# First attention: the projection of q directly behind that of the context's keys, the turned inverse sums behind both

## The chip, the cores and the metric

The kernel runs on one core of a Trainium2 chip. The metric is the device time of one launch in microseconds (us): 1333.4 us before the change, the median of three runs from 1332.63 to 1336.6 us. One further execution was profiled; all rows below are from it.

## What is computed

The input x is 32 entries of 128 tokens by 128 channels, with a context of 120 tokens per entry. Four blocks follow one another, each added to x. Only the first one is touched:

```
x = x + _L0_xattn_ref(ctx_1024, _layernorm(x), mask, ...)      # the first attention
x = x + _L0_ffn_ref(_layernorm(x), ...)
x = x + _L1_xattn_ref(_layernorm(x), ctx_1024, ctx_1024, ...)
x = x + _L1_ffn_ref(_layernorm(x), ...)

# inside the first attention, 8 heads of 64:
q = latents @ Wq                                   # latents: the normed tokens of x
k, v = split(concatenate([ctx, latents]) @ Wkv)    # 120 + 128 = 248 keys
q = l2norm(q) * q_scale;  k = l2norm(k) * k_scale
attn = softmax(where(mask, q @ k.T * 8, -max))
out = layer_norm((attn @ v) @ Wo) 
```

## The kernel before, in words

`l0_attention` works through the 32 entries one at a time, in a software pipeline written out by hand. Each engine has its own list of steps, `body(n, par)`, which `run_steps` calls for n from -2 to 33; a step for entry n + 2 (the projections), one for n + 1 (turning q and the keys, the first scores) and those for n (softmax and the product with the values) stand side by side in one body. Each engine takes its list strictly in the order written; semaphores with names like `q_proj` or `vl_copied` count entries done, and a step begins with its waits. The eight PSUM banks are shared by the steps under fixed rules; bank 7, for one, holds in turn the values of x, q, and the keys of x.

TensorE's steps that matter here (names of the functions, with the lines of their matmuls):

- `project_kc` (L334): the context's keys of entry n + 2, 512 wide, into bank 6. It waits for `kvT_made`, that is for ScalarE's two copies of the turned inputs (L496, L497).
- `turn_sums` (L426): two transposes of `r_wide`, the inverse sums of the softmax of entry n repeated over 64 columns, into bank 4. It waits for `sum_repeated` (VectorE, L624) and for `pt0_copied` (ScalarE's copy L541, which empties bank 4). u is the half of the heads, 0 or 1; the change touches u = 0.
- `project_q` (L340): q of entry n + 2, 512 wide, into bank 7. It waits for `kvT_made` and for `vl_copied`, since bank 7 still holds the values of x of entry n + 1 until ScalarE has copied them (L489, `copy_values_x`).
- `multiply_v` (L441), `turn_probs0` (L407), `turn_kc` (L352), `project_kl` (L345, the keys of x, into bank 7 once `q_copied` is there), `turn_probs1` (L418), `turn_kl` (L367), `turn_q` (L360), `multiply_v` and `turn_sums` of the other half, `values_c` (L374), `scores` (L392, L397), `values_x` (L381), `scores`, `project` (L450).

ScalarE's list runs: copy of the context's values (L483), four exponentials of half 0 (L533), copy of the output projection (L553), the two copies that make `kvT` (L496, L497), `copy_pt0` (L541), `copy_values_x` (L489), four exponentials of half 1, `copy_sums` of half 0 (L547, waits for the turned sums), the copies of the context's keys and of q (L504, twice), `copy_pt0`, `copy_kcT` (L518), the copy of the keys of x (L504), the squares (L512), `copy_qT` (L315), `copy_sums` of half 1. A product in float32 stands in the trace as two loads of weights and two matmuls; a transpose as one of each.

The waits of the three steps that change their neighbours, as the code has them:

```
def project_q(m):
    if there(m):
        wait(pe, s["kvT_made"], m + 1)
        wait(pe, s["vl_copied"], m)
def turn_sums(n, u):
    if there(n):
        wait(pe, sum_repeated[u], n + 1)
        wait(pe, pt0_copied[u], n + 1)
```

Of the kernel before, what the change touches and what calls it, by code (L numbers as in the profile page):

```python
# [30 lines left out]
def wait(eng, sem, value):  # L31

    if isinstance(value, int) and value <= 0:
        return
    eng.wait_ge(sem, value)  # L35
# [103 lines left out]
def there(n):  # L139

    return not isinstance(n, int) or 0 <= n < B


def l0_attention(nc, psum, X, stats6, mean, rstd, mhalf, small, ident, ident_bf, ones, cols,
# [6 lines left out]
    with ExitStack() as sems, ExitStack() as st:  # L151
# [169 lines left out]
        with nc.Block() as block:  # L321
            @block.tensor
            def _(pe):
                def turn_inputs(m):
                    if there(m):
                        wait(pe, s["ln_made"], m + 1)
                        wait(pe, s["vc_copied"], m)
                        pe.transpose(psum[:, 6, 0:C], ln_c[0:C, :], ident[0:C, 0:C])
                        pe.transpose(psum[:, 6, P:2 * P], ln_x[:, :], ident[:, :]).then_inc(s["ln_turned"], 1)

                def project_kc(m):
                    if there(m):
                        wait(pe, s["kvT_made"], m + 1)
                        pe.matmul(psum[0:C, 6, :], kvT[:, 0:C], wkv[:, 0:INNER], start=True, stop=True).then_inc(s["kc_proj"], 1)  # L334
# [5 lines that stand above are left out]
                        pe.matmul(psum[:, 7, :], kvT[:, C:K], wq[:, :], start=True, stop=True).then_inc(s["q_proj"], 1)  # L340

                def project_kl(m):
                    if there(m):
                        wait(pe, s["q_copied"], m + 1)
                        pe.matmul(psum[:, 7, :], kvT[:, C:K], wkv[:, 0:INNER], start=True, stop=True).then_inc(s["kl_proj"], 1)  # L345

                def turn_kc(m):
                    if there(m):
                        wait(pe, s["normed"], m + 1)
                        wait(pe, s["kc_copied"], min(m + 2, B) if isinstance(m, int) else m + 2)  # L350
                        for c in range(4):
                            tr = pe.transpose(psum[:, 6, c * C:(c + 1) * C], qkn[0:C, 1, c * P:(c + 1) * P], ident[0:C, 0:C])  # L352
                        tr.then_inc(s["kcT_turned"], 1)
# [22 lines left out]
                def values_x(m):  # L376
                    if there(m):
                        wait(pe, s["qT_copied"], m)
                        wait(pe, s["qT_scaled"], m)
                        wait(pe, s["kl_copied"], m + 1)  # L380
                        pe.matmul(psum[:, 7, :], kvT[:, C:K], wkv[:, INNER:], start=True, stop=True).then_inc(s["vl_proj"], 1)  # L381

                def scores(n, u, par):
                    if there(n):
                        if u == 0:
                            wait(pe, s["qT_copied"], n + 1)
                            wait(pe, s["qT_scaled"], n + 1)
                            wait(pe, s["klT_copied"], n + 1)
                            wait(pe, s["keep_copied"], n + 1)
                        wait(pe, exp_done[u], n)  # L390
                        for r in range(2):
                            pe.matmul(psum[:, 2 * u + r, 0:2 * K], first_row[64 * r:64 * r + 64, :],  # L392
                                      keep_now[par][64 * r:64 * r + 64, :].unsqueeze(1).broadcast_to([64, 2, K]),
                                      start=True, stop=False, skip_group_check=True)
                        for j in range(2):
                            for r in range(2):
                                mm = pe.matmul(psum[:, 2 * u + r, j * K:(j + 1) * K], QT[par][64 * r:64 * r + 64, 2 * u + j, :],  # L397
                                               KT[par][64 * r:64 * r + 64, 2 * u + j, :], start=False, stop=True,
                                               skip_group_check=True)
                        mm.then_inc(scored[u], 1)  # L400

                def turn_probs0(n, u):
                    if there(n):
                        wait(pe, exp_done[u], n + 1)
                        wait(pe, r_copied[1 - u], n if u == 0 else n + 1)
                        for j in range(4):
                            tr = pe.transpose(psum[0:C, 4, j * P:(j + 1) * P], probs[u][:, j, 0:C], ident[:, :])  # L407
                        tr.then_inc(pt0_turned[u], 1)

                def turn_probs1(n, u):  # L410
                    if there(n):
                        wait(pe, exp_done[u], n + 1)
                        if u == 0:
                            wait(pe, s["projection_taken"], n)
                        else:
                            wait(pe, out_scaled[0], n + 1)
                        for j in range(4):
                            tr = pe.transpose(psum[:, 5, j * P:(j + 1) * P], probs[u][:, j, C:K], ident[:, :])  # L418
                        tr.then_inc(pt1_turned[u], 1)
# [5 lines that stand above are left out]
                        for b in range(2):  # L425
                            tr = pe.transpose(psum[:, 4, b * P:(b + 1) * P],  # L426
                                              r_wide[u][:, 2 * b:2 * b + 2, :].rearrange("p h w -> p (h w)"), ident[:, :])
                        tr.then_inc(r_turned[u], 1)

                def multiply_v(n, u, par):  # L430
                    if there(n):
                        wait(pe, pt0_copied[u], n + 1)
                        wait(pe, pt1_copied[u], n + 1)
                        if u == 0:
                            wait(pe, s["vc_copied"], n + 1)
                            wait(pe, s["vl_copied"], n + 1)
                        for j in range(2):
                            for part, V, rows in ((0, VC, C), (1, VL, P)):
                                for r in range(2):
                                    h = 4 * u + 2 * j + r  # L440
                                    mm = pe.matmul(psum[HD * r:HD * r + HD, 5, j * P:(j + 1) * P], V[par][0:rows, h * HD:(h + 1) * HD],  # L441
                                                   probsT[u][0:rows, part, 2 * r + j, :], start=(part == 0), stop=(part == 1),
                                                   skip_group_check=True)
                        mm.then_inc(pv_done[u], 1)

                def project(n):
                    if there(n):
                        wait(pe, out_scaled[1], n + 1)
                        for c in range(4):
                            mm = pe.matmul(psum[:, 5, 0:D], outT[:, c, :], wo[:, c, :], start=(c == 0), stop=(c == 3))  # L450
                        mm.then_inc(s["projected"], 1)

                def body(n, par):
                    values_x(n + 1)
                    scores(n, 1, par)
                    project(n - 1)
                    turn_inputs(n + 2)
                    turn_probs0(n, 0)
                    turn_probs1(n, 0)
                    project_kc(n + 2)  # L460
                    turn_sums(n, 0)
                    project_q(n + 2)
                    multiply_v(n, 0, par)
                    turn_probs0(n, 1)
                    turn_kc(n + 1)
                    project_kl(n + 2)
                    turn_probs1(n, 1)
                    turn_kl(n + 1)
                    turn_q(n + 1)
                    multiply_v(n, 1, par)  # L470
                    turn_sums(n, 1)
                    values_c(n + 2)
                    scores(n + 1, 0, 1 - par)

                run_steps(pe, body)

            @block.scalar
# [1731 lines left out]
```

## Time and profile before

| | |
|---|---|
| median of 3 runs | 1333.4 us (1332.63 to 1336.6) |
| the profiled execution | 1335.86 us, its span 1333.7 us |
| TensorE (PE) | matmuls on record for 1230.1 us, 92% of the span |
| loads of weights (PEld) | 879.3 us, 66% |
| VectorE (DVE), ScalarE (ACT), GpSimd (POOL) | 70%, 60%, 44% |
| first attention | about 28 to 510 us of the span |
| granted TensorE clock, mean | 0.969 of full speed |

The profiled execution's own time is 2.5 us above the median; the span leaves out another 2.2 us around it. "Busy" on PE covers each matmul from its start until its modelled end, and matmuls overlap, so a PE that is busy all the time may still have paused between two of them; the pauses show in the starts of the rows, and in the idle time of PEld.

### The profile page before, as it was taken

The page shows a single profiled execution, that of the slowest core. Times are in us where ns is not written, and L with a number is a line of the kernel's source. Part 1 is how long each engine was busy: PE and PEld are TensorE (multiplying, and loading weights), DVE is VectorE, ACT ScalarE, POOL GpSimd, SP SyncE. Part 2 cuts the span into 40 slices and gives each one's busy share as a digit, 9 for nine tenths or more (in the row PEclk, how much of TensorE's full clock was granted, in tenths as well). Part 3 has the DMA queues.
Part 4 walks back from the last instruction along what each step waited for, and adds up shares of the span by engine and source line. Part 5 has one row for each costly group of instructions (what it writes and reads, how often), then busy time and mean ns, then how long its engine had stood idle before and what let it go on. Part 6 is the DMA issues. An engine that isn't in the chain of part 4 may idle for free. (4 is left out here: it accounts for less than half of the span.)

```text
span 1333.7 us, 37978 instructions
## 1 busy us (share of the span) xinstructions
PE 1230.1 (92%) x13719; PEld 879.3 (66%) x13719; DVE 927.5 (70%) x2003; ACT 798.9 (60%) x2101; POOL 588.9 (44%) x673
## 2 busy tenths in 40 slices
PE   1899999999999995978999899989999979999996
PEld 0466666666666663436777777768888847777775
DVE  6476676677677673766999889979999955343431
ACT  0578878878878862325777677756666633333332
POOL 3577566666656655104223332343333223333343
PEclk9899999999999997987999899989999979999998
DMA  8000000000000000000000002000000000000000
GB/s 216 13 1 1 0 0 0 0 0 0 0 0 0 0 1 1 0 4 10 11 9 8 10 10 69 3 2 1 0 0 0 0 1 9 9 8 8 8 11 16
DMA packets 22740, 14.71 MB, mean 11 GB/s; under 512 B 6378, under 2 KB 21610, under 8 KB 22540
## 3 DMA queue, kind: packets, MB, share of 16 engines
q1 hardware_dynamic: 22520, 13.75, 3.8%
q8 instruction: 43, 0.70, 0.2%
q14 instruction: 29, 0.24, 0.1%
q10 hardware_dynamic: 148, 0.01, 0.0%
HBM read 11.66 MB, written 2.10 MB: 10 GB/s over the span
## 5 line engine op out<-in xcount | busy, mean ns | idle before, releaser
L690 POOL TENSOR_TENSOR r_norm<-ssm,mhalf 128x24 f32<-128x24 f32 x32 | 134.9, 4215 | 162.7 <-DVE ssm L595 162.7
L1767 POOL TENSOR_TENSOR pair_QX<-pair_qT,own_slots 128x512 f32<-128x512 f32 x64 | 66.7, 1041 | 257.7 <-ACT pair_qT L1579 257.7
L1985 ACT ACTIVATE moe_hid<-psum 128x512 f32<-128x512 f32 x128 | 76.4, 598 | 137.5 <-PE psum L1919 137.5
L1525 PE MATMUL psum<-ident,pair_probs 128*120 128x128 f32 (+1 forms) x1024 | 154.6, 285 | 0.7 <-ACT pair_probs L1594 0.6
L533 ACT ACTIVATE l_probs<-psum,l_n_max 128x248 f32<-128x248 f32 x256 | 117.2, 481 | 57.7 <-DVE l_n_max L613 57.7
L2143 POOL TENSOR_TENSOR moe_acc<-moe_acc,moe_prod 128x512 f32<-128x512 f32 x64 | 81.3, 1271 | 147.4 <-DVE moe_prod L2099 147.4
L1594 ACT ACTIVATE pair_probs<-psum,pair_n_max 128x120 f32<-128x120 f32 (+1 forms) x512 | 137.7, 380 | 10.4 <-DVE pair_n_max L1636 5.0
L1929 PEld LDWEIGHTS psum<-w,moe_hid 128*128 128x128 f32 x1024 | 123.1, 192 | 26.8 <-issue 26.8
L2099 DVE TENSOR_TENSOR moe_prod<-psum,moe_combine 128x512 f32<-128x512 f32 x64 | 44.3, 692 | 135.8 <-PE psum L1929 135.7
L1525 PEld LDWEIGHTS psum<-ident,pair_probs 128*120 128x120 f32 (+1 forms) x1024 | 111.3, 141 | 28.6 <-issue 11.9
L1462 ACT COPY pair_probsT<-psum 120x512 f32<-120x512 f32 (+1 forms) x128 | 77.7, 607 | 86.4 <-PE psum L1525 86.2
L1929 PE MATMUL psum<-w,moe_hid 128*128 128x128 f32 x1024 | 123.4, 275 | 0.0
L1919 PE MATMUL psum<-moe_moe_hT,w 128*128 128x512 f32 x256 | 122.5, 606 | 0.0
L1536 PE MATMUL psum<-pair_probsT,V 120*32 120x128 f32 (+1 forms) x2048 | 107.2, 281 | 0.3 <-DVE X L1678 0.3
L1539 PE MATMUL psum<-pair_probsT,ONE 120*32 120x128 f32 (+1 forms) x2048 | 104.3, 275 | 0.0
L1462 DVE COPY pair_probsT<-psum 120x512 f32<-120x512 f32 (+1 forms) x128 | 87.2, 681 | 4.7 <-PE psum L1525 4.6
L697 POOL TENSOR_TENSOR qkn<-qk,r_norm 128x1536 f32<-128x1536 f32 x32 | 88.4, 2762 | 2.5
L1602 ACT ACTIVATE pair_probs<-pair_probs 128x960 f32<-128x960 f32 (+1 forms) x64 | 67.0, 1047 | 35.9 <-DVE pair_probs L1654 35.9
L1636 DVE TENSOR_REDUCE pair_n_max<-psum 128x8 f32<-128x960 f32 (+1 forms) x64 | 76.1, 1189 | 8.8 <-PE psum L1514 8.8
L640 DVE TENSOR_TENSOR outT<-psum,r_spread 128x256 f32<-128x256 f32 x64 | 26.9, 420 | 78.8 <-PE psum L441 73.3
L613 DVE TENSOR_REDUCE l_n_max<-psum 128x4 f32<-128x992 f32 x64 | 76.3, 1192 | 6.4 <-PE psum L397 2.4
L1514 PE MATMUL psum<-pair_kT,pair_QX 32*128 32x120 f32 (+1 forms) x2048 | 77.2, 287 | 0.0
(292 smaller groups left out, 2925.3 us busy)
## 6 DMA issues: line engine op xcount, KB each, us to landing
X<-x_in SPq DMA_DIRECT2D x8, 256.0 KB, 4.6
out_dram<-moe_acc SPq DMA_DIRECT2D x32, 64.0 KB, 1.5
CT<-ctx_in SPq DMA_DIRECT2D x8, 240.0 KB, 5.5
pair_cT<-ctxT_in SPq DMA_DIRECT2D x32, 60.0 KB, 1.8
w<-w_in SPq DMA_DIRECT2D x1, 1024.0 KB, 5.0
wm<-wm_in SPq DMA_DIRECT2D x1, 768.0 KB, 4.3
wp<-wp_in SPq DMA_DIRECT2D x1, 768.0 KB, 6.6
wkv<-wkv_in SPq DMA_DIRECT2D x1, 512.0 KB, 5.3
```

What stands on the lines that cost most here:

```text
L533: e = act.activation(probs[u][:, h, :], psum[:, 2 * u + h // 2, (h % 2) * K:(h % 2 + 1) * K], ACT.Exp, bias=n_max[u][:, h:h + 1], accum_ou ...
L690: pool.tensor_tensor(r_norm[:, :], ssm[:, :], mhalf[:, 0:3 * H], ALU.pow).then_inc(s["norm_inverted"], 1)
L697: pool.tensor_tensor(qkn[:, :, :].rearrange("p a (h d) -> p (a h) d", d=HD), qk[:, :, :].rearrange("p a (h d) -> p (a h) d", d=HD), r_norm ...
L1462: copy(probsT[0:K, g, :, :], psum[0:K, 4 + g % 2, :].rearrange("k (j q) -> k j q", j=4)).then_inc(copied[g], 1)
L1514: mm = pe.matmul(psum[:, t, s * K:(s + 1) * K], QX[par][32 * t:32 * t + 32, s, :], kT[par][32 * t:32 * t + 32, 0:K], start=False, stop=(s ...
L1525: tr = pe.transpose(psum[0:K, 4 + g % 2, j * P:(j + 1) * P], probs[par][:, 4 * g + j, 0:K], ident[:, :])
L1536: pe.matmul(psum[32 * tile:32 * tile + 32, 6, 0:P], V[par][0:K, g * P + 32 * tile:g * P + 32 * tile + 32], probsT[0:K, g, tile, :], start= ...
L1539: mm = pe.matmul(psum[32 * tile:32 * tile + 32, 6, P:2 * P], ONE[0:K, 32 * g:32 * g + 32], probsT[0:K, g, tile, :], start=False, stop=(g = ...
L1594: e = act.activation(probs[par][:, h, 0:K], psum[:, h // 4, (h % 4) * K:(h % 4 + 1) * K], ACT.Exp, bias=n_max[par][:, h:h + 1])
L1919: pe.matmul(psum[:, 2 + i % BANKS, :], w1[:, e, half * P:(half + 1) * P], hT[par][:, :], start=True, stop=True).then_inc(hidden[i], 1)
L1929: mm = pe.matmul(psum[:, 5 + e % 2, b * D:(b + 1) * D], hid[i % RING][:, b * P:(b + 1) * P], w2[:, i, :], start=(half == 0), stop=(half == ...
L2143: pool.tensor_tensor(a[:, :, :], a[:, :, :], prod[e % 2][:, :, :], ALU.add).then_inc(summed[e], 1)
```

## The change

`project_q(n + 2)` and `turn_sums(n, 0)` change places in TensorE's list. No instruction is added or removed, and no wait is changed.

```
--- before.py
+++ after.py
@@ -458,8 +458,8 @@
                     turn_probs0(n, 0)
                     turn_probs1(n, 0)
                     project_kc(n + 2)
+                    project_q(n + 2)
                     turn_sums(n, 0)
-                    project_q(n + 2)
                     multiply_v(n, 0, par)
                     turn_probs0(n, 1)
                     turn_kc(n + 1)
```

TensorE, the middle of one body (psum<-wkv,kvT is the product for the context's keys, psum<-wq,kvT that for q, r_wide the repeated inverse sums):

```order
 L418 MATMUL psum<-ident,l_probs 128x128 x4
 L334 MATMUL psum<-wkv,kvT 120x512
-L426 MATMUL psum<-ident,r_wide 128x128 x2
 L340 MATMUL psum<-wq,kvT 128x512
+L426 MATMUL psum<-ident,r_wide 128x128 x2
 L441 MATMUL psum<-l_probsT,VC 64x128 x2
 L441 MATMUL psum<-l_probsT,VL 64x128 x2
```

The two transposes moved from ahead of the product for q to behind it. The same piece stands eight times in the code that is built (six written-out bodies and the two of the loop), and in the execution it runs for 30 entries.

ScalarE's list beside it, the same before and after, from the copies that make kvT to the copy of the keys of x:

```order
 L497 ACTIVATE kvT<-psum,cols 128x128
 L541 COPY l_probsT<-psum 120x512
 L489 COPY VL<-psum 128x512
 L533 ACTIVATE l_probs,l_sums<-psum,l_n_max 128x248 x4
 L547 COPY r_spread<-psum 128x256
 L504 COPY qk<-psum 120x512
 L504 COPY qk<-psum 128x512
 L541 COPY l_probsT<-psum 120x512
 L518 COPY KT<-psum 128x4x120
```

Nothing moved here. L489 is what the product for q waits for, L547 what waits for the turned sums, and the second L504 what empties q's bank.

## Rows read from the trace of the kernel before

**Rows 1.** The page: busy us, share of the span, instructions.
```profile
PE 1230.1 (92%) x13719; PEld 879.3 (66%) x13719; DVE 927.5 (70%) x2003; ACT 798.9 (60%) x2101; POOL 588.9 (44%) x673
```

**Rows 2.** Stretches in the first attention: busy us by engine, granted clock, DMA share, GB/s.
```profile
100.00:200.00 100.00, 99.93 (x723) 64.48 (x722) 69.80 (x147) 79.43 (x215) 65.86 (x52) 1.00 0.00 1
200.00:300.00 100.00, 99.95 (x725) 64.75 (x725) 70.02 (x145) 79.21 (x215) 62.94 (x50) 1.00 0.00 0
```

**Rows 3.** The product for q (L340), whole run: count, ns min/median/max, first and last start.
```profile
L340 PEld LDWEIGHTS psum<-wq,kvT x64: 190/192/337, 28.9 to 476.9; 128*128 128x128 f32 x64
```

**Rows 4.** The first product (L334), 100 to 340 us, the same columns.
```profile
L334 PEld LDWEIGHTS psum<-wkv,kvT x34: 179/180/183, 100.9 to 331.7; 128*120 128x120 f32 x34
```

**Rows 5.** Timeline of one entry: start us, us, engine, line [idle before <-releaser].
```profile
215.75 0.45 ACT L497 ACTIVATE kvT<-psum,cols 128x128 f32<-128x128 f32 x1
...
216.25 0.28 PEld L334 LDWEIGHTS psum<-wkv,kvT 128*120 128x120 f32 x2 [0.26 <-ACT kvT L497]
216.25 1.12 PE L334 MATMUL psum<-wkv,kvT 128*120 128x512 f32 x2
...
216.56 0.60 ACT L489 COPY VL<-psum 128x512 f32<-128x512 f32 x1
216.79 0.14 PEld L426 LDWEIGHTS psum<-ident,r_wide 128*128 128x128 f32 x1 [0.25 <-issue]
217.04 0.49 ACT L533 ACTIVATE l_probs<-psum,l_n_max 128x248 f32<-128x248 f32 x1
217.21 0.38 PE L426 MATMUL psum<-ident,r_wide 128*128 128x128 f32 x2
217.21 0.14 PEld L426 LDWEIGHTS psum<-ident,r_wide 128*128 128x128 f32 x1 [0.28 <-issue]
217.32 0.30 PEld L340 LDWEIGHTS psum<-wq,kvT 128*128 128x128 f32 x2
...
217.43 1.02 PE L340 MATMUL psum<-wq,kvT 128*128 128x512 f32 x2
...
218.38 0.44 PE L441 MATMUL psum<-l_probsT,VC 120*64 120x128 f32 x4
```

**Rows 6.** The same entry, ScalarE's copies behind the exponentials, and TensorE there.
```profile
218.82 0.42 ACT L547 COPY r_spread<-psum 128x256 f32<-128x256 f32 x1
...
219.07 1.14 ACT L504 COPY qk<-psum 120x512 f32<-120x512 f32 x2
...
219.41 0.65 PE L407 MATMUL psum<-ident,l_probs 128*120 128x128 f32 x4
...
219.90 0.58 PE L352 MATMUL psum<-ident,qkn 120*128 120x120 f32 x4
...
220.26 0.30 PEld L345 LDWEIGHTS psum<-wkv,kvT 128*128 128x128 f32 x2
...
221.23 0.60 PE L418 MATMUL psum<-ident,l_probs 128*128 128x128 f32 x4
```

**Rows 7.** The same entry, the turning of q (L360) behind the copy of the keys of x.
```profile
221.48 0.59 ACT L504 COPY qk<-psum 128x512 f32<-128x512 f32 x1 [0.32 <-PE psum L345]
221.66 0.60 PE L367 MATMUL psum<-ident,qkn 128*128 128x128 f32 x4
...
222.18 0.42 PEld L360 LDWEIGHTS psum<-ident,qkn 128*128 128x128 f32 x4 [0.16 <-issue]
```

**Rows 8.** Who waited for whom, 100 to 340 us: us in total, times, longest.
```profile
POOL r_norm L690 <- DVE ssm L595: 79.7, 17, 5.0
```

More of the change, by code:

```diff
@@ L460, in body @@
                     project_kc(n + 2)
+                    project_q(n + 2)
                     turn_sums(n, 0)
-                    project_q(n + 2)
                     multiply_v(n, 0, par)
```

## The prediction

> **What bounds the kernel now.** I read the page first, then the stretches of the first attention, then one entry of it row by row. The page gives TensorE 92% of the span [rows 1]. In the first attention it is on record all the time, 99.9 us of every 100, at the full granted clock of 1.00 (2.4 GHz), while ScalarE has 79% and VectorE 70% [rows 2]. GpSimd waits 79.7 us in 17 entries for VectorE, so it has time to spare [rows 8]. One entry takes (331.7 - 100.9) / 16 = 14.4 us: the first and last start of L334 in the stretch, for 34 loads, two per entry, the second a tenth behind the first [rows 4]. So the time of this stage is the sum of what TensorE streams and of its short pauses, and I read those from the distance between starts. What the change costs or saves per entry counts in full, unless another engine's fixed chain takes it up. L340 has 64 loads, so 32 entries [rows 3]; for the first two no inverse sums are turned, which leaves 30.
>
> **The change part by part.** Nothing is added or removed: two transposes and one product of 512 columns change places. What has to be priced is which of them meets its waits at what time.
>
> *How TensorE goes through the place now.* ScalarE finishes kvT at 215.75 + 0.45 = 216.20, the load for L334 starts at 216.25, and the first transpose of the sums at 217.21 [rows 5]. The load for that transpose starts at 216.79, as the second pass of L334 begins, 0.42 to 0.43 before 217.21; so a pass takes 0.43, a product 0.86, and what is left of the 0.96 from load to successor is 0.10, the load that stands in the open because it had to wait. Behind it there is no gap: the two transposes take 217.43 - 217.21 = 0.22, the product for q runs from 217.43 to about 218.29, and L441 starts at 218.38 after 0.09 for the switch to its shape.
>
> *The product for q, moved forward.* It may not start before ScalarE has emptied its bank: L489 runs from 216.56 to 216.56 + 0.60 = 217.16 [rows 5]. TensorE would be free for it at 217.21, but wants the load before that, at 216.79 (where the sums' load stands now); it can't have it. The transposes hid this wait: they needed nothing from L489 and filled 0.22. From the end of a ScalarE copy to the load it releases I see 0.05 (kvT, 216.20 to 216.25; and the copy of q, which ends at 219.07 + 1.14 = 220.21, to the load of L345 at 220.26 [rows 6]) and 0.11 (the keys of x, 221.48 + 0.59 = 222.07 to the load of L360 at 222.18 [rows 7]). L360 waits for two semaphores, as L340 does, while L334 and L345 wait for one; so I take 0.11. The Trainium skill, page "Perfetto Trace Analysis", section "Identifying Dependency Chains", says that an instruction waiting for several engines may get a semaphore instruction ahead of it; that is one way to read the difference, and no number here hangs on it.
>
> So the load for q starts at 217.16 + 0.11 = 217.27, and its columns stream from 217.37, against 217.21 for what stands there now: **0.16 us later**. With a hand-over of 0.05 it is 0.10 later. Then 0.86 and 0.22 as before, and L441 starts at 218.54 instead of 218.38. Nothing behind the waiting load is blocked for another reason; the sums and L441 are ready, they are only late with it.
>
> *The transposes of the sums, moved back.* They now end at 217.21 + 0.38 = 217.59; then at 217.37 + 0.86 + 0.38 = 218.61. Their reader, L547, starts at 218.82, behind ScalarE's exponentials [rows 6]. Even with a hand-over of 0.11 that is in time: cost nothing. If the exponentials were shorter by more than 0.1 us, this copy, and the two L504 behind it, would slip. The product for q ends earlier than now, but its copy stands behind the same exponentials: gain nothing.
>
> *What takes some of it back.* L345 is held by the copy of q: the four transposes of L352 begin at 219.90 and are through after about 0.41 (0.58 less one transpose's length of 0.27, plus 0.10 for its columns), at 220.31, while the load at 220.26 lets L345 stream from 220.36 only, and L418 follows at 221.23. This chain on ScalarE (L489, exponentials, L547, L504 twice) hangs on nothing that the change moves, so a TensorE that comes 0.16 later loses this 0.05 again. Every other wait of the entry (0.26 for kvT, 0.1 for the keys of x at L360) starts from a product of TensorE itself, moves with it, and takes up nothing. GpSimd's spare time hides its part.
>
> The sum: 0.16 - 0.05 = **0.11 us per entry, times 30 = 3.3 us**. The profiled execution's 1335.86 us would become 1339.2; against the median of 1333.4 us, which I forecast, it is **1336.7 us**. The bounds: 0.10 - 0.05 = 0.05 per entry gives 1.5 us, 0.16 with nothing taken back gives 4.8 us.
>
> **A rule that speaks against a cost.** The trace shows the load of the sums' transpose at 216.79 beside the second pass of L334, both on all 128 rows, and the transpose 0.42 later with no gap [rows 5]; so loads do hide here, and one that has to wait does not. The Trainium skill, page "TensorE: Matmul & The Clock Gate", section "The mechanism", says that a load of weights overlaps running matmuls only when its group of rows is another one. By that rule the load would be in the open in either order and only the late hand-over would count; rival 1 has its time.
>
> **The rivals.**
> 1. *The move is free.* The load for q costs the same wherever it stands, so the wait costs 217.27 - 217.21 = 0.06, and L345's 0.05 takes that back: 0.01 x 30 = 0.3 us, 1333.7. For it: L489 ends 0.05 before TensorE wants the bank. Against it: the hidden load at 216.79.
> 2. *Slower by more than can be overlooked.* The load for q stands in the open with its whole recorded length, 0.19 [rows 3], instead of 0.10: columns from 217.46, 0.25 late, 0.20 after what is taken back, times 30 = 6.0 us, 1339.4. It decides from 0.13 us per entry on (4.0 us in all). Against it: L334's load is recorded with 0.18 too [rows 4], and its successor comes after 0.96, not 1.04.
> 3. *Faster.* The load side sits idle for 0.25 and 0.28 around the sums' transposes [rows 5]. If the second of these were a true pause between two kinds of matmul, and two products back to back spared it, an entry would gain 0.28 - 0.11 = 0.17, times 30 = 5.1 us: 1328.3. Against it: the starts of the matmuls leave no room for a pause.
> 4. *The order on TensorE is not what decides*, because ScalarE's chain sets the entry. Then nothing changes: 1333.4. Against it: TensorE's waits that ScalarE releases are themselves released by TensorE.
>
> **How the numbers follow.** A measurement of this kernel tells about 0.3%, 4.0 us, from no change. Forecast: chance 0.57; with its bounds of 1.5 to 4.8 us and runs that differ by a few us, about a quarter of it lies above 4.0. Rival 1: 0.16. Rival 2: 0.17. Rival 3: 0.04. Rival 4: 0.06. So faster 0.04; slower 0.17 + 0.15 = 0.32; within 0.3% the rest, 0.64. The later stages are untouched and only start some 3 us later. The likeliest is 1336.7 us. The range of 1333.0 to 1340.0 us holds the forecast with both bounds, rival 1 and 4, and rival 2 at its price.
>
> **What would show it.** In the profile of the changed kernel L334 is followed by the load of L340, about 1.02 us behind the load of L334 (217.27 - 216.25) and 0.11 behind the end of L489, not 0.5 behind L334's; L426 about 1.98 behind it, L441 2.29 instead of 2.13. L345's load no longer starts 0.05 behind the end of the copy of q but later. L547 keeps its place at 2.57 behind L334's load. The entry takes 14.5 us instead of 14.4, and the stage ends some 3 us later. If the entry takes 14.4 as before, rival 1 or 4 holds, and the place of L441 tells which; if L441 comes at 2.38 or later, rival 2; if L441 comes before 2.13, rival 3. A start of L547 behind 2.57 would mean that I mispriced the late sums.

## The result, and the profile after

The change makes the kernel slower by a quarter of a per cent: 1337.43 us, the median of 18 runs (1334.11 to 1339.34), against 1334.06 us, the median of 18 runs of the kernel before. The ratio is 1.0024, with a 95% interval from 1.0017 to 1.0031. That is 2.3 to 4.1 us, where 3.3 were forecast. The forecast of 1336.7 us started from the 1333.4 us of three runs; from the 1334.06 of 18 the same 3.3 give 1337.4. The 18 runs resolve a difference that lies below the 0.3% set as the bound of "no change".

The page of the changed kernel shows nothing of it but the span; TensorE's share is the same [rows 1]:

```profile
span 1336.7 us, 37978 instructions
PE 1230.6 (92%) x13719; PEld 878.4 (66%) x13719; DVE 923.2 (69%) x2003; ACT 801.7 (60%) x2101; POOL 588.4 (44%) x673
```

Nor do the stretches of the first attention, which answer to [rows 2] (busy us by engine, granted clock, DMA share, GB/s). TensorE is on record all the time with and without the longer pause, and at the same clock:

```profile
100.00:200.00 100.00, 99.93 (x716) 64.05 (x716) 68.09 (x145) 79.25 (x210) 64.98 (x52) 1.00 0.00 1
200.00:300.00 100.00, 99.95 (x724) 64.62 (x720) 68.21 (x146) 80.57 (x217) 62.11 (x49) 1.00 0.00 0
```

The starts tell it. The loads of L334 from 100 to 340 us (count, ns min/median/max, first and last start), and those of L340 in the whole run, answer to [rows 4] and [rows 3]:

```profile
L334 PEld LDWEIGHTS psum<-wkv,kvT x34: 179/180/183, 101.1 to 333.8; 128*120 128x120 f32 x34
...
L340 PEld LDWEIGHTS psum<-wq,kvT x64: 186/189/337, 29.9 to 480.2; 128*128 128x128 f32 x64
```

34 loads are 17 entries, so 16 distances and the 0.1 us between the two loads of one product: (333.8 - 101.1 - 0.1) / 16 = 14.54 us per entry, against (331.7 - 100.9 - 0.1) / 16 = 14.42 before. 0.12 us more, 30 times, is 3.6 us. (From 101.1 to the last load of L334 at 479.2 us it is 378.1 us, before from 100.9 to 475.8 374.9: 3.2 us more for 26 entries. The first 70 us of the stage differ by 0.8 us the other way between these two single executions, which was not looked into.) This length of an entry is what the experiments below are read by, since it is steadier than a time: it is worked out in the same way for each.

One entry, from the timeline of the changed kernel (start us, us, engine, line, [idle before <-releaser]), answers to [rows 5, 6]:

```profile
202.38 0.45 ACT L497 ACTIVATE kvT<-psum,cols 128x128 f32<-128x128 f32 x1
...
202.88 0.28 PEld L334 LDWEIGHTS psum<-wkv,kvT 128*120 128x120 f32 x2 [0.23 <-ACT kvT L497]
...
203.19 0.61 ACT L489 COPY VL<-psum 128x512 f32<-128x512 f32 x1
...
203.91 0.30 PEld L340 LDWEIGHTS psum<-wq,kvT 128*128 128x128 f32 x2 [0.74 <-issue]
203.94 1.10 PE L340 MATMUL psum<-wq,kvT 128*128 128x512 f32 x2
...
204.87 0.38 PE L426 MATMUL psum<-ident,r_wide 128*128 128x128 f32 x2
...
205.19 0.44 PE L441 MATMUL psum<-l_probsT,VC 120*64 120x128 f32 x4
...
205.45 0.42 ACT L547 COPY r_spread<-psum 128x256 f32<-128x256 f32 x1
...
205.70 1.15 ACT L504 COPY qk<-psum 120x512 f32<-120x512 f32 x2
...
206.71 0.57 PE L352 MATMUL psum<-ident,qkn 120*128 120x120 f32 x4
...
207.02 0.30 PEld L345 LDWEIGHTS psum<-wkv,kvT 128*128 128x128 f32 x2
...
207.98 0.60 PE L418 MATMUL psum<-ident,l_probs 128*128 128x128 f32 x4
```

Counted from L334's load, in us, before (from [rows 5, 6], with L334 at 216.25) and after:

| | before | after | forecast |
|---|---|---|---|
| the copy of the values of x (L489) ends | 0.91 | 0.92 | as before |
| load of the product for q (L340) | 1.07 | 1.03 | 1.02 |
| first transpose of the sums (L426) | 0.96 | 1.99 | 1.98 |
| first product with the values (L441) | 2.13 | 2.31 | 2.29 |
| copy of the turned sums (L547) | 2.57 | 2.57 | 2.57 |
| load for the keys of x (L345) | 4.01 | 4.14 | later than 4.01 |
| L418, behind it | 4.98 | 5.10 | 0.11 later |

The load for q stands 0.11 us behind the end of the copy that it waits for, and not 0.42 ahead of its columns as the load of the transposes did. At L441 the entry is 0.17 to 0.18 behind; from L345 on it is 0.12 behind, since that load no longer waits for the copy of q (which ends at 205.70 + 1.15 = 206.85) but follows the transposes of L352.

### The profile page after: what moved, and what is told of

It reads as the page before. It is cut to its first block and busy times, and to the rows that moved or that the text cites. A ratio compares the mean times of both kernels' runs of the same rounds, so it can differ in the third digit from the quotient of the medians.

```text
span 1336.7 us, 37978 instructions
## 1 busy us (share of the span) xinstructions
PE 1230.6 (92%) x13719; PEld 878.4 (66%) x13719; DVE 923.2 (69%) x2003; ACT 801.7 (60%) x2101; POOL 588.4 (44%) x673
## 5 line engine op out<-in xcount | busy, mean ns | idle before, releaser
L613 DVE TENSOR_REDUCE l_n_max<-psum 128x4 f32<-128x992 f32 x64 | 76.2, 1191 | 6.6 <-PE psum L397 2.6
```

## The experiments

Ten kernels were run, each against the kernel before on the same chip. An entry of each is worked out from the loads of L334, as above.

### The wait taken away: ScalarE copies the values of x first

The edit, on the changed kernel, in ScalarE's list:

```
-                    copy_pt0(n, 0)
                     copy_values_x(n + 1, 1 - par)
+                    copy_pt0(n, 0)
```

> The changed kernel, but ScalarE copies the values of x (L489) ahead of the probabilities (L541), so the bank for q is free some 0.47 us earlier. My theory (the product for q waits for that copy and its load then stands in the open): the wait is gone, L426 about 1.82 us behind L334's load and L441 at 2.13 as before the change, L345's load 0.05 behind the copy of q again, an entry 14.42 us, ratio to before 1.000. Rival (the place of the transposes between the two products is what matters, not the wait): L441 stays at 2.30, an entry 14.54 us, ratio 1.0024.

Measured: 1334.05 us, ratio 0.9998 (0.9988 to 1.0009); the entry (331.6 - 100.9 - 0.1) / 16 = 14.41. From its timeline:

```profile
201.67 0.58 ACT L489 COPY VL<-psum 128x512 f32<-128x512 f32 x1
201.83 0.28 PEld L334 LDWEIGHTS psum<-wkv,kvT 128*120 128x120 f32 x2 [0.23 <-ACT kvT L497]
...
202.37 0.19 PEld L340 LDWEIGHTS psum<-wq,kvT 128*128 128x128 f32 x1 [0.25 <-issue]
202.78 1.02 PE L340 MATMUL psum<-wq,kvT 128*128 128x512 f32 x2
...
203.64 0.38 PE L426 MATMUL psum<-ident,r_wide 128*128 128x128 f32 x2
```

The load for q now stands 0.54 behind L334's and its columns follow at 0.95, the places that the sums had in the kernel before. The order of the change is kept, and its cost is gone. The order as such costs nothing; the wait does.

### The same swap in the kernel before

> The kernel before, with the same swap on ScalarE. Now the transposes of the sums meet the late copy (L541 ends about 0.90 us behind L334's load). My theory: their load starts at 1.01 instead of 0.53, their columns 0.11 late, 0.05 of it taken back at L345: an entry 14.48 us, plus 1.8 us in all, ratio 1.0013. Rival (the order on TensorE alone matters): nothing changes, ratio 1.000.

The edit is the same, made on the kernel before. Now the copy of the probabilities, which the sums wait for, is the late one. Measured: 1336.61 us, ratio 1.0016 (1.0005 to 1.0027); the entry (333.8 - 101.9 - 0.1) / 16 = 14.49.

```profile
203.65 0.60 ACT L541 COPY l_probsT<-psum 120x512 f32<-120x512 f32 x1
204.37 0.20 PEld L426 LDWEIGHTS psum<-ident,r_wide 128*128 128x128 f32 x2 [0.74 <-issue]
204.40 0.41 PE L426 MATMUL psum<-ident,r_wide 128*128 128x128 f32 x2
```

The copy ends at 204.25, the load follows 0.12 later and 1.02 behind L334's load at 203.35. L441 starts 2.25 behind L334's load instead of 2.13, so the sums' columns start at 0.96 + 0.12 = 1.08: ahead of transposes the load stands 0.06 in the open, not 0.10 as ahead of a product. The 0.12 less the 0.05 at L345 is the loss of the entry, 0.07 us, 0.06 forecast: it appears in the old order. The two runs cross: with ScalarE's old order TensorE's old order is the better one by 0.12, with ScalarE's new order the new one is, by 0.08.

### The price of the second wait

```
                 def project_q(m):
                     if there(m):
-                        wait(pe, s["kvT_made"], m + 1)
                         wait(pe, s["vl_copied"], m)
```

> The changed kernel, but the product for q waits for the copy of the values alone; that kvT is made was waited for by the product just ahead of it on the same engine. My theory (two waits cost 0.11 us from the end of the copy to the load, one costs 0.05): q's load 0.96 instead of 1.03 behind L334's, L441 at 2.24, L345's 0.05 still taken back, an entry 14.48 us, ratio to before 1.0012. Rival (the hand-over has nothing to do with the number of waits): as the change, ratio 1.0024, load at 1.03.

Measured: 1336.83 us, ratio 1.0013 (1.0002 to 1.0024); the entry (333.7 - 102.0 - 0.1) / 16 = 14.48. Line numbers are one lower here (L339 is the product for q, L488 the copy of the values of x):

```profile
203.32 0.28 PEld L334 LDWEIGHTS psum<-wkv,kvT 128*120 128x120 f32 x2 [0.23 <-ACT kvT L496]
...
204.29 0.30 PEld L339 LDWEIGHTS psum<-wq,kvT 128*128 128x128 f32 x2 [0.68 <-ACT VL L488]
204.29 1.12 PE L339 MATMUL psum<-wq,kvT 128*128 128x512 f32 x2
```

The load comes 0.97 behind L334's instead of 1.03, and half of what the change costs is gone. So a wait that was long met was part of this step's hand-over. The profile tells the two cases apart too: with one wait it names ScalarE's copy as what ended the idle time, with two it says "issue". The number of waits alone is not the rule, though. In `project_q` the late wait is the second of the two in the code; the last two sections have a step whose first wait is the late one, and there the hand-over is 0.05 with both waits in place.

### What came back at the keys of x

Both of the next kernels let VectorE copy the turned sums of half 0 (L547 before), so that ScalarE reaches the copy of q earlier:

```
+                def copy_sums0(n):
+                    if there(n):
+                        wait(dve, r_turned[0], n + 1)
+                        wait(dve, out_scaled[1], n)
+                        dve.tensor_copy(r_spread[:, :, :], psum[:, 4, 0:2 * P]...).then_inc(r_copied[0], 1)
```

> The kernel before, but VectorE instead of ScalarE copies the turned sums of half 0 (L547), so ScalarE reaches the copy of q some 0.25 us earlier. My theory (L345 is held about 0.05 us by the copy of q, and by nothing else): its columns start 0.05 earlier, an entry 14.36 us, ratio to before 0.9988. Rival (the copy of q holds nothing): 14.42, 1.000.

> The changed kernel with the same move of the copy to VectorE. My theory (the change costs 0.17 at the product for q, and 0.05 of it came back at L345 because that was held anyway): with the hold gone on both sides nothing comes back, an entry 14.53 us as in the change, 0.17 more than the kernel before with the same move, ratio to before 1.0024. Rival (the 0.12 between before and change is all that the late product costs): 0.12 more than that kernel, 14.48, ratio 1.0015.

Measured: on the kernel before 1333.41 us, ratio 0.9994 (0.9984 to 1.0004), the entry (332.1 - 102.1 - 0.1) / 16 = 14.37; on the change 1336.68 us, ratio 1.0026 (1.0016 to 1.0036), the entry (334.7 - 102.0 - 0.1) / 16 = 14.54. On the first, L345's load comes 3.96 behind L334's, where it was 4.01:

```profile
202.72 0.28 PEld L334 LDWEIGHTS psum<-wkv,kvT 128*120 128x120 f32 x2 [0.23 <-ACT kvT L497]
...
205.29 1.12 ACT L504 COPY qk<-psum 120x512 f32<-120x512 f32 x2
...
206.68 0.30 PEld L345 LDWEIGHTS psum<-wkv,kvT 128*128 128x128 f32 x2
```

With the hold gone on both sides the orders are 0.17 apart, not 0.12. So the late product for q costs 0.17, and 0.05 of it fell into a wait that the kernel before had anyway. The times alone would not have shown the 0.05 (1.5 us in 30 entries); the entries do.

### The lesson used elsewhere: the sums of the other half

TensorE pauses at L360 for ScalarE's copy of the keys of x [rows 7]. On the kernel before:

```
                     turn_kl(n + 1)
+                    turn_sums(n, 1)
                     turn_q(n + 1)
                     multiply_v(n, 1, par)
-                    turn_sums(n, 1)
```

> The kernel before, but the turned sums of the other half stand ahead of the turning of q (L360), where TensorE pauses about 0.14 us for the copy of the keys of x. My theory (a short ready piece ahead of a step that waits hides the wait): the pause goes, the values product L374 starts 0.10 us earlier behind L334's load (7.72 instead of 7.82; the load behind the products with 64 columns is now its own 0.10 in the open), an entry 14.32 us, minus 3.0 us, ratio 0.9977. Rival (the pause is only moved: another wait from ScalarE or VectorE ends as late as before): an entry 14.42, ratio 1.000.

Measured: 1329.87 us, ratio 0.9968 (0.9955 to 0.998); the entry (330.9 - 101.7 - 0.1) / 16 = 14.32.

```profile
207.19 0.59 ACT L504 COPY qk<-psum 128x512 f32<-128x512 f32 x1 [0.32 <-PE psum L345]
...
207.38 0.60 PE L367 MATMUL psum<-ident,qkn 128*128 128x128 f32 x4
...
207.81 0.38 PE L426 MATMUL psum<-ident,r_wide 128*128 128x128 f32 x2
207.92 0.47 PEld L360 LDWEIGHTS psum<-ident,qkn 128*128 128x128 f32 x4
...
208.03 0.60 PE L360 MATMUL psum<-ident,qkn 128*128 128x128 f32 x4
```

The copy ends at 207.78, while TensorE is busy with the turned sums; the load of L360 follows at 207.92, 0.11 ahead of its first transpose. Nothing pauses: 0.43, 0.22 and then L360. The entry is 0.10 shorter, as worked out; that is 3.0 us in all, while the medians are 4.2 apart, with 3.0 inside the interval. It is the mirror image of the change: a short piece that is ready stands ahead of one that is not.

### kvT on VectorE: a miss

The largest pause of an entry is that of 0.26 ahead of L334 [rows 5]. Both copies that make kvT were given to VectorE, between its maximum (L613) and the inverse sums; the sums of the other half stand ahead of L360 as above.

```
                     maximum(n, 1)
+                    make_kvT(n + 2)
                     invert_sums(n, 0)
```

with, in `make_kvT`, `tensor_scalar(..., LNX_W, LNX_B, ALU.mult, ALU.add)` and its like for the tokens. It was run with TensorE's old order (first) and with that of the change (second).

> The kernel before with the sums of the other half ahead of the turning of q, and with both copies that make kvT on VectorE instead of ScalarE; ScalarE's list is shorter by two copies. My theory: the pause of 0.26 us ahead of L334 goes, and with it the hold at L345, an entry 14.32 - 0.26 - 0.05 = 14.01 us, minus 12 us in all, ratio 0.9908. Rival (VectorE, which now has the two copies ahead of the inverse sums and the other copies, ends later than TensorE needs it, and the pause comes back at the products with the values): 14.3 us, 0.997.

> The same with the order of the change, the product for q directly behind that for the context's keys. My theory (what the order costs is how far the copy of the values of x lies behind the moment the load for q could start): the copy ends about 0.63 us behind the place of L334's load as it is now, the load follows at 0.74 where it could start at 0.27, the columns at 0.84 instead of 0.70: 0.14 more than the same kernel with the old order, nothing taken back, an entry 14.15 us, ratio 0.994. Rival (with ScalarE's list shorter by two copies the values of x are copied in time): no difference between the two orders.

Measured: 1395.09 us, ratio 1.0472 (1.0432 to 1.0511), the entry (335.4 - 104.4 - 0.1) / 14 = 16.49; and 1407.09 us, ratio 1.0551 (1.0533 to 1.0569), the entry (328.9 - 106.2 - 0.1) / 13 = 17.12. Neither theory had this. Who waited for whom from 100 to 340 us, in the first of them (line numbers shifted: L622 is VectorE's copy into r_wide, L624 before), and one entry:

```profile
PEld psum L426 <- DVE r_wide L622: 37.6, 15, 2.5
...
PE psum L426 <- DVE r_wide L622: 25.0, 15, 1.7
```

```profile
217.54 0.40 DVE L581 TENSOR_SCALAR kvT<-psum,cols 128x120 f32<-128x120 f32 x1
...
217.86 0.40 DVE L582 TENSOR_SCALAR kvT<-psum,cols 128x128 f32<-128x128 f32 x1
...
218.14 2.76 POOL L696 TENSOR_TENSOR qkn<-qk,r_norm 128x1536 f32<-128x1536 f32 x1
...
218.38 2.67 DVE L622 COPY r_wide<-l_r_sums 128x256 f32<-128x256 f32 x1
...
221.10 0.20 PEld L426 LDWEIGHTS psum<-ident,r_wide 128*128 128x128 f32 x2 [2.50 <-DVE r_wide L622]
```

In the kernel before, the same copies, of both halves, with GpSimd beside them:

```profile
215.42 0.29 DVE L624 COPY r_wide<-l_r_sums 128x256 f32<-128x256 f32 x1
...
215.91 2.76 POOL L697 TENSOR_TENSOR qkn<-qk,r_norm 128x1536 f32<-128x1536 f32 x1
...
216.31 0.69 DVE L632 COPY l_probsT<-psum 128x512 f32<-128x512 f32 x1
...
219.90 0.47 POOL L721 TENSOR_TENSOR y_wb<-y_w,lnob 128x128 f32<-128x128 f32 x1
...
220.07 0.45 DVE L624 COPY r_wide<-l_r_sums 128x256 f32<-128x256 f32 x1
```

The copy of 128x256 took 2.67 us. In the kernel before that of half 0 takes 0.29, and it starts some 0.5 us ahead of GpSimd's qkn. Here the two kvT copies push it behind the start of qkn, and it ends at 221.05, 0.15 behind the end of qkn (220.90). The copy of the other half shows the same on a small scale in the kernel before: it starts beside GpSimd's y_wb, takes 0.45 and ends at 220.52, again 0.15 behind the end of y_wb (220.37). TensorE waits for the late copy with the sums.

In the second kernel the product for q goes ahead of the sums and TensorE waits less in one piece, yet it is slower still. What the order was forecast to cost there, 0.14, did not come: the copy of the values of x ends 0.73 behind L334's load, q's load follows at 0.85 and its columns at 0.96, where TensorE is free for them anyway. The difference lies in the granted clock, 0.95 from 100 to 350 us against 0.99 in the first. In the second kernel it falls to 0.50 of full speed (1.2 GHz) for some 3.4 us in every second entry (from 213.2 to 216.6 us, for one), seven times from 100 to 340 us, and such an entry takes 1.5 us longer; in the first it falls twice, and those entries take 1.6 to 1.7 longer. Without these falls the entries would be about 16.3 and 16.25 us, by my estimate from these numbers. Ahead of the fall at 213.2 TensorE stood still for 0.81 us for the sums and for 0.92 ahead of L441; one entry later it stood still for 0.81 and 1.02 (up to 229.29 and 230.75), and the clock stayed at full speed. Why it fell in one entry and not in the next stays open.

### The copy into r_wide on ScalarE

```
-                    dve.tensor_copy(r_wide[0] ..., r_sums[0] ...)     (invert_sums, u == 0)
+                    act.copy(r_wide[0] ..., r_sums[0] ...)            (repeat_sums0, ahead of exponentials(n, 1))
```

In both kernels ScalarE copies the values of x before the probabilities; they differ in TensorE's order alone, which is that of the change in the first and the old one in the second. (The expectation for the second speaks of ScalarE's old order. The kernel that ran has the new one.)

> As e8 (kvT on VectorE, the order of the change, the sums of the other half ahead of the turning of q), but the inverse sums of half 0 are repeated into r_wide by ScalarE instead of VectorE, behind the copies of the values of x and of the probabilities. My theory (the 2.7 us that VectorE's copy into r_wide took in e7 is a lock-out by GpSimd's qkn, which runs from 218.14 to 220.90 there and which the copy met only because the kvT copies pushed it back; with no such copy in that stretch the loss goes): an entry about 14.05 us, minus 11 us in all, ratio to before 0.992. Rival (VectorE simply has too much to do since it makes kvT): an entry stays above 15 us, ratio above 1.03.

> The same division of the work, with the old order (the sums ahead of the product for q) and ScalarE's old order of the two copies. Here the sums become ready last, at about 0.62 us behind the place of L334's load, where their load could start at 0.27. My theory (whichever of the two is ready first belongs ahead; here that is q): the columns of the sums start about 0.08 late, an entry 14.13 us, 0.08 more than e9, ratio 0.994. Rival (the old order is better by 0.12 whatever is ready first): 13.93 us.

Measured: 1327.59 us, ratio 0.9953 (0.9939 to 0.9966), the entry (328.7 - 101.8 - 0.1) / 16 = 14.18; and 1325.35 us, ratio 0.9939 (0.9923 to 0.9956), the entry (327.4 - 100.4 - 0.1) / 16 = 14.18. From the first:

```profile
214.70 0.40 DVE L591 TENSOR_SCALAR kvT<-psum,cols 128x128 f32<-128x128 f32 x1
...
214.99 2.76 POOL L707 TENSOR_TENSOR qkn<-qk,r_norm 128x1536 f32<-128x1536 f32 x1
...
215.16 0.28 PEld L334 LDWEIGHTS psum<-wkv,kvT 128*120 128x120 f32 x2 [0.18 <-DVE kvT L591]
215.30 0.41 ACT L532 COPY r_wide<-l_r_sums 128x256 f32<-128x256 f32 x1
```

From the second, where the sums stand ahead of the product for q:

```profile
213.83 0.28 PEld L334 LDWEIGHTS psum<-wkv,kvT 128*120 128x120 f32 x2 [0.18 <-DVE kvT L591]
...
213.97 0.41 ACT L532 COPY r_wide<-l_r_sums 128x256 f32<-128x256 f32 x1
...
214.43 0.14 PEld L426 LDWEIGHTS psum<-ident,r_wide 128*128 128x128 f32 x1 [0.32 <-ACT r_wide L532]
...
214.79 0.38 PE L426 MATMUL psum<-ident,r_wide 128*128 128x128 f32 x2
```

ScalarE's copy into r_wide takes 0.41 us in the middle of qkn, and the entry is 2.3 us shorter than that of the kernel above with the same order of TensorE (16.49) in the one case, 2.9 (17.12) in the other. VectorE's work is otherwise as it was: it lost a copy of 0.29 us. So it was the meeting of that copy with qkn, not the amount of VectorE's work. The size of the gain was off: 14.18 instead of 14.05, because VectorE needs 214.39 to 215.10, 0.71 us, for the two copies and ScalarE's pair took 0.80; L334 still pauses. For the same reason the difference of 0.08 between the two orders did not come: counted from L334's real place, the copy into r_wide ends at 0.55 and the copy of the values of x before it. The first order meets no wait. In the second the load of the sums comes at 0.60 instead of 0.54, still 0.36 ahead of its columns at 0.96: a load that is late and yet hidden costs nothing. Both kernels beat the kernel before and the change; whether the 0.9939 is really better than the 0.9953 is open, the intervals overlap and the entries are equal.

These rows also correct the price of the second wait. `turn_sums` waits first for the repeated sums, then for the copy of the probabilities. Here the first is the late one, and the load follows it by 0.05 (214.38 to 214.43); likewise by 0.05 (221.05 to 221.10) where VectorE made the sums late. In the swap on the kernel before, the second was the late one, and the same load came after 0.12. In `project_q` and `turn_q` (L360) the late wait is also the second. So the 0.06 was paid where the late wait stands behind another in the code, and not wherever a step has two. That writing the late wait first would save it without dropping any follows from this, but no kernel tried it.

## Why the prediction was right

- *What bounds the stage.* TensorE's own sequence does: each of the kernels that lengthened or shortened one pause there moved the entry by that pause, less what fell into the hold at L345, also where ScalarE had less to do (the entry of 14.54 with the sums on VectorE).
- *The hand-over.* 0.11 from the end of the copy to the load with two waits, taken from L360 and not from L334: measured 203.91 - 203.80 = 0.11. The reason was only half right. That it hangs on the number of waits was a reading of three rows; dropping the met wait took 0.06 off, so the second wait is shown to cost that in this step. But L426 has two waits as well and follows in 0.05 when the first of them is the late one. And both waits of L340 are for copies of ScalarE, so it is not a matter of waiting for several engines. The number came out because L340 and L360, from which it was taken, both have the late wait second.
- *The load in the open.* Columns 0.10 behind the load: L426 stands 204.87 - 203.91 = 0.96 behind q's load, 0.86 of it streaming. Rival 2, with the whole 0.19 in the open, is out.
- *The loss at L441.* Forecast 0.16, measured 0.17 to 0.18 in the rows.
- *What comes back.* Forecast 0.05 at L345, measured 0.17 less 0.12, and shown by the pair with the sums on VectorE.
- *The late sums.* Priced at nothing: L547 keeps its 2.57, although the transposes end at 204.87 + 0.38 = 205.25, only 0.2 ahead of it.
- *The sum.* 0.12 per entry instead of 0.11, so 3.6 us by the entries, and 3.4 by the medians, against 3.3.
- Rival 1 (free) and the rule behind it, that a load hides only beside matmuls on other rows, are out: the load's move from hidden to open is 0.10 of the 0.17. Rival 3 is out, since with the wait gone the new order gives 14.41 and not less. Rival 4 is out by the same runs as the first point.

## What to carry to other kernels

In a list that an engine takes in order, put ahead of a step that waits for a bank or a copy the short piece that is already ready, even if its result is not wanted yet; compare, for each, the end of what it waits for with the moment its load of weights could start, since that load is what goes into the open first. A wait that the step ahead on the same engine has already met can be dropped; it saved 0.06 us where the load stood in the open, and nothing is to be expected where the load is hidden. When a copy on VectorE moves in time, look at what GpSimd is doing at its new time.

## What the runs showed of the hardware

- A load of weights that doesn't wait stands ahead of the matmul it serves, beside a matmul on the same 128 rows: 0.42 where a product of 512 columns goes ahead of that matmul, 0.11 where transposes do (L340 in the kernel before). One that waits costs 0.10 ahead of a product and 0.06 ahead of the transposes of the sums (128 columns, float32). The sentence of the Trainium skill ("TensorE: Matmul & The Clock Gate", section "The mechanism") that loads overlap only where the row group differs does not hold for these rows. The same section also allows a load into the background weight buffer, and that case they fit.
- From the end of a copy to the load that it releases: 0.05 us with one wait, and with two where the late one stands first in the code (L426); 0.11 to 0.12 where the late one stands second (L340, L360, L426), although the other is long met. Dropping the met one took the load from 1.03 to 0.97 behind L334's.
- VectorE's copy from one SBUF tile to another, 128x256 in float32, takes 0.29 us alone and 2.67 us when it starts 0.24 us behind a GpSimd operation that runs for 2.76; the same copy on ScalarE takes 0.41 beside it. The lost time is recorded as the copy's own. VectorE's copy of 512 columns out of PSUM (L632) takes 0.69 beside qkn, and 0.69 at 221.87 with no qkn there. The Trainium skill, page "SBUF — State Buffer", section "Who interferes with whom", says that VectorE in a two-port mode and GpSimd share a pair of ports and that the second to start is blocked until the first is through; this trace agrees, with the copy's end 0.15 us behind that of qkn, and behind that of y_wb in the other half. The mode itself is not recorded.
- TensorE's granted clock fell to 0.50 (1.2 GHz) for some 3.4 us, costing 1.5 to 1.7 us each time, behind pauses of 0.81 and 0.92 us in one entry, and not behind those of 0.81 and 1.02 in the next (the kernel with kvT on VectorE and the order of the change).
